# Reading all 47 block experts into TensorE's registers during the second shared chunk instead of one per routed block

## What is computed

```
shared = (silu(x @ sfc1.T) * (x @ sfc2.T)) @ sfc3.T        # 256 -> 512 -> 256
top_w, top_idx = top_k(x @ gate_w.T, 2);  top_w = softmax(top_w)
h   = silu(einsum('td,ehd->teh', xf, w1))                  # 256 -> 128 per expert
moe = einsum('teh,te,edh->td', h, dispatch, w2)            # 128 -> 256 per expert
x   = x + tanh(g_ffn[3]) * (moe + shared)
```

## Time and profile before

| what | value |
|---|---|
| runs | 2107.64, 2121.74, 2106.2 us |
| median | 2107.64 us |
| span of the profiled execution | 2103.8 us |
| mean granted TensorE clock in it | 0.915 |
| TensorE matmul busy | 1757.4 us, 84% |
| VectorE busy | 1144.3 us, 54% |
| ScalarE busy | 890.7 us, 42% |
| GpSimd busy | 861.0 us, 41% |

### The profile page before, as it was taken

One profiled execution on the slowest core, in us unless ns is written; L12 is line 12 of the kernel. 1 busy time (PEld: TensorE's weight loads), 2 busy tenths in 40 slices (PEclk: granted clock), 3 DMA queues, 4 the chain that ended last, 5 costly groups with the idle time before them and its releaser, 6 DMA issues.

```text
span 2103.8 us, 25825 instructions
## 1 busy us (share of the span) xinstructions
PE 1757.4 (84%) x9054; PEld 1079.5 (51%) x9054; DVE 1144.3 (54%) x2206; ACT 890.7 (42%) x1397; POOL 861.0 (41%) x810
## 2 busy tenths in 40 slices
PE   6936999959867888839996987999999999967985
PEld 3426899837643222434553664544555554543652
DVE  5742544478795776722225696556565556452224
ACT  3312443323378877611212664555544445410530
POOL 2162112124595544430004463566565566725022
PEclk9767999989987999969998987999999999989997
DMA  9531322020000000340113000000000000022442
GB/s 354 182 101 55 119 100 100 19 100 1 20 1 1 6 6 5 124 171 28 37 36 98 1 1 31 1 1 0 1 1 1 1 1 1 1 88 83 135 129 83
DMA packets 62742, 116.75 MB, mean 55 GB/s; under 512 B 8240, under 2 KB 51492, under 8 KB 60057
## 3 DMA queue, kind: packets, MB, share of 16 engines
q1 hardware_dynamic: 54552, 94.92, 13.0%
q0 software_dynamic: 8064, 20.19, 2.9%
HBM read 71.22 MB, written 44.89 MB: 55 GB/s over the span
## 4 chain that ended last, share of the span: by engine, by line
PE 64%; DVE 14%; ACT 6%; POOL 6%; issue 5%; another core or an unknown queue 3%; DMA 2%; SPq 0%; POOLq 0%; ACTq 0%; DVEq 0%
PE psum L151 61%; POOL arena L1777 3%; DVE arena L2311 2%; ACT arena L1567 2%; DVE arena L156 1%; POOL xb L1030 1%; DVE arena L2375 1%; DVE arena L172 1%; DMA arena<-xb 1%; POOL arena L1786 1%; DVE arena L2318 1%; DVE rounded L898 1%; PE psum L667 1%; DVE arena L1155 1%
## 5 line engine op out<-in xcount | busy, mean ns | idle before, releaser
L151 PE MATMUL psum<-arena 128*64 128x512 f32 (+21 forms) x5109 | 1191.5, 463 | 178.2 <-issue 24.9
L151 PEld LDWEIGHTS psum<-arena 128*128 128x128 f32 (+8 forms) x5109 | 569.1, 165 | 684.8 <-issue 465.9
L151 PE MATMUL psum<-rounded 128*128 128x270 f32 (+6 forms) x2688 | 486.0, 334 | 27.6 <-DVE rounded L898 19.6
L151 PEld LDWEIGHTS psum<-rounded 128*128 128x128 f32 (+3 forms) x2688 | 379.1, 187 | 134.6 <-issue 44.8
L2403 POOL TENSOR_TENSOR arena<-arena 128x1024 f32<-128x1024 f32 (+1 forms) x112 | 265.8, 2374 | 133.8 <-ACT arena L2353 131.6
L2353 ACT ACTIVATE arena<-psum 128x1024 f32<-128x1024 f32 x144 | 147.4, 1024 | 172.0 <-PE psum L151 171.3
L2311 DVE TENSOR_REDUCE arena<-psum 128x1 f32<-128x512 f32 x256 | 163.6, 682 | 90.4 <-PE psum L151 89.3
L1567 ACT ACTIVATE arena<-psum,arena 128x1024 f32<-128x1024 f32 (+1 forms) x192 | 156.5, 911 | 46.5 <-PE psum L151 46.4
L850 POOL DMA_INDIRECT arena<-yb,arena x48 | 46.1, 960 | 266.3 <-DMA yb<-arena 252.8
L1793 POOL TENSOR_TENSOR arena<-arena 128x256 f32<-128x256 f32 x128 | 95.8, 770 | 117.7 <-ACT arena L1567 116.9
L1183 POOL DMA_INDIRECT yt<-arena x40 | 39.9, 998 | 208.0 <-DVE arena L1146 205.8
(11 more groups left out here) (268 smaller groups left out, 1951.8 us busy)
## 6 DMA issues: line engine op xcount, KB each, us to landing
arena<-in_w SPq DMA_DIRECT2D x8, 2048.0 KB, 7.8
arena<-xb SPq DMA_DIRECT2D x70, 128.0 KB, 2.2
yb<-arena SPq DMA_DIRECT2D x70, 128.0 KB, 1.7
arena<-in_w1u SPq DMA_DIRECT2D x4, 2048.0 KB
xb<-arena SPq DMA_DIRECT2D x3, 2048.0 KB, 15.9
xb<-arena SPq DMA_DIRECT2D x2, 2064.0 KB, 32.6
arena<-xb SPq DMA_DIRECT2D x8, 516.0 KB
yt<-arena SPq DMA_DIRECT2D x2, 2048.0 KB, 16.6
```

Of the source, the lines that this page charges most:

```text
L151: return e.matmul(o, l, r, start=start, stop=stop, skip_group_check=True)
```

## The change

`pe_shared` takes an additional argument `between`, a function that it calls after each `mm`. For chunks 0, 2 and 3 it does nothing. For chunk 1 it is `next_expert`, which loads the next entry of `ER` into a register of its own: 16 calls fall behind the up matmuls and 16 behind the down matmuls. The 15 entries that are left are loaded after the chunk, one behind another, ahead of the wait for `s_hs` and of `turn(0)`. The first call waits for `s_er`, a wait that stood ahead of the loop before. In the loop, `up(j)` loads nothing any more; `up` and `down` use the same register values as before. No other engine's stream is changed.

```diff
--- before.py
+++ after.py
@@ -2585,7 +2585,7 @@
                     e.dma_start(yb3[128 * (j - 2):128 * (j - 2) + 128, :], f3_Y[:, (j - 2) % 3, :]).then_inc(
                         s_rout[(j - 2) % 3], 16)
 
-        def pe_shared(e, c):
+        def pe_shared(e, c, between=lambda: None):
             for f in range(4):
                 n = 4 * c + f
                 b1 = 2 * (n % 2) + 2
@@ -2596,6 +2596,7 @@
                     for k in range(2):
                         m = mm(e, psum[:, b1 + i, :], w[:, k, 128 * f:128 * f + 128], XT[:, k, 512 * c:512 * c + 512],
                                k == 0, k == 1)
+                        between()
                     m.then_inc(s_up, 1)
             for t in range(4 * c, 4 * c + 4):
                 e.wait_ge(s_hs, 4 * c + 4)
@@ -2647,8 +2649,20 @@
             pe_totals(e, 16, 32, f3_w)
             e.wait_ge(s_w3, 32)
             e.wait_ge(s_slot, 5)
-            for c in range(2):
-                pe_shared(e, c)
+            pe_shared(e, 0)
+            regs = []
+
+            def next_expert():
+
+                if len(regs) < NB3:
+                    if not regs:
+                        e.wait_ge(s_er, 2)
+                    n = len(regs)
+                    regs.append(e.value_load(ER[0:1, n:n + 1], min_val=0, max_val=15))
+
+            pe_shared(e, 1, next_expert)
+            while len(regs) < NB3:
+                next_expert()
 
             def turn(j):
                 e.wait_ge(s_rin[j % 4], RIN3[j % 4] + 16 * (j // 4 + 1))
@@ -2662,7 +2676,6 @@
                 e.wait_ge(s_bx, 23 + j + 1)
                 if j >= 2:
                     e.wait_ge(s_bh_, 23 + j - 1)
-                regs[j] = e.value_load(ER[0:1, j:j + 1], min_val=0, max_val=15)
                 for k in range(2):
                     m = mm(e, psum[:, 2 + j % 2, 0:128], f3_XGT[:, j % 3, k, :],
                            f3_W1[:, bass.ds(regs[j], 1), k, :].rearrange("p e n -> p (e n)"), k == 0, k == 1)
@@ -2680,12 +2693,10 @@
                 mm(e, psum[:, 6 + j % 2, 0:256], f3_HTT[:, j % 2, :],
                    f3_W2[:, bass.ds(regs[j], 1), :].rearrange("p e n -> p (e n)"), True, True).then_inc(s_bd, 1)
 
-            regs = {}
             e.wait_ge(s_hs, 8)
             turn(0)
             turn(1)
             e.wait_ge(s_wm, 208)
-            e.wait_ge(s_er, 2)
             for j in range(NB3 + 2):
                 if j < NB3:
                     up(j)
```

## The result

| | kernel before | changed kernel |
|---|---|---|
| median of 16 runs each | 2108.38 us | 2118.85 us |
| lowest to highest | 2102.69 to 2121.74 | 2112.25 to 2127.26 |
| span of the profiled execution | 2103.8 us | 2116.0 us |

The ratio of changed to before is 1.0041, with a 95% interval of 1.0023 to 1.0059: 8.6 us slower, 4.8 to 12.4. The medians are 10.5 us apart. The forecast of 2118 and its sign hold. All ratios in this document leave out two disturbed executions of over 4000 us, one of the kernel before and one of e6.

A forecast was written before the change was run, and what follows sets the result against it. TensorE's sequencer, with one register load a block, was taken to bound the routed blocks. Moved loads 14.7 plus clock 2.7 minus loop gain 7.3 gave 10.1 us later, span 2113.9, forecast 2118 us; range for all 2107 to 2126.

The forecast's parts named there:

- What bounds the blocks before: In the 47 routed blocks, TensorE's sequencer with one register load a block sets the pace, 1.59 us on average.
- What is late next: In the blocks without loads, row loads queued behind stores on SP: 4.04 us per three blocks, 1.35 a block.
- The gain: In the block loop: 46 x (1.53 - 1.35) - 1.0 = 7.3 us saved, bounds zero and 17.8.
- What the moved loads cost: In and behind the second shared chunk: 0.65 us a load, so the blocks begin 14.7 us later; bounds 9.1 and 18.1.
- 16 loads behind the up matmuls cost nothing: In the second shared chunk, 0.65 us a load fits under a 0.86 us matmul pair; without cover 10.4 us.
- The clock: First blocks: about 10 us idle cools the array to half clock for 5.4 us, costing 2.7; bounds nothing and 5.4.
- Nothing behind the blocks changes: Behind the last block: gathers move with the blocks' end, so its gain or loss passes on unchanged.
- The sum: Whole kernel: 14.7 + 2.7 - 7.3 = 10.1 us later, all on the path, a span of 2113.9.
- overlapping loads: Rival, in the 31 loads behind 1943.61: only 0.17 us paid each, blocks start no later, 2100 us; chance 0.06.
- blocks that stay near 1.59: Rival, in the loop: values don't stay in registers or landings lengthen, no gain, 2125 us; chance 0.12.
- a clock of 1.2 GHz through the blocks: Rival, in the blocks: TensorE stays at 1.2 GHz, 38 us more, 2150 us or over; chance 0.05.
- a block bound by the array: Rival, in the blocks: array binds at 1.20 to 1.30 us, not rows; 2107 to 2115, named 2111; chance 0.17.

The follow-up runs named there:

- e6: Kernel before, each block's expert load without its run-time bounds check (no register arithmetic or assertion): 2066.43 us against 2070.26, ratio 0.9980.
- e4: Kernel before, with each row load in SyncE's stream issued one step earlier: 2106.58 us, ratio 0.9984.
- e3: Changed kernel, with each row load in SyncE's stream issued one step earlier: 2112.32 us against the changed kernel's 2118.85.
- clean pair: Kernel before and changed kernel, both unedited, run again under other conditions: 2069.26 and 2078.95 us, ratio 1.0046.
- e2: Changed kernel, 47 loads placed elsewhere: 12 behind first chunk's up matmuls, 19 ahead of its last tile, 16 behind second chunk's up matmuls: 2116.92 us, ratio 1.0040.
- e5: Changed kernel, with the run-time bounds check of each loaded expert left out: 2072.63 us, ratio to the kernel before 1.0006.
- e7: Kernel before, all 47 experts read by three multi-register loads without bounds check ahead of the first turn: 2073.62 us, ratio 1.0015.
- e8: Changed kernel, an unread dummy matmul call behind each of the last 15 loads: one execution, S to end 182.77 us against 182.45.
- e12: Same kernel as e2, no edit, run again under the other conditions: 2074.43 us, ratio to the kernel before 1.0019.
- first group: Profiles taken under one group of conditions; under the other, every kernel that ran in both was 38 to 43 us shorter.
- e11: Kernel before, with e6's load without bounds check and e4's earlier row loads: 2055.04 us against 2069.26, ratio 0.9919.

## Why the prediction was right, point by point

- **What bounds the blocks before** (the sequencer): right. e6 takes only sequencer work out and gains 5.6 us; e4 makes rows earlier and gains 2.9.
- **What is late next** (rows, 4.04 us per three blocks): right. It is 4.10 between the turns at 2008.37, 2012.47 and 2016.57, and e3 takes this limit away and reaches 1.26 a block. The mean is 1.42 with the long landings. The gain, 7.3 forecast, was 7.7 and, in the clean pair, 7.45. So near a hit is in part luck: in the five other kernels whose blocks load no expert and keep the order of the row loads (e2, e5, e7, e8, e12) the blocks take 65.9 to 68.4 us, a gain of 4.6 to 7.0 over the kernel before of the same group. Their length goes with TensorE's waits for rows: its weight loads wait 7.0 us in the changed kernel (65.27) and 10.8 in e2 (68.44). I had charged 1.0 us for the long landings and not asked what makes them. The traces tell: they show 322 row loads of the blocks with their landings. In flight with 58 of them was a packet of 16384 bytes that the profile calls "instruction", on queue 8. Those loads took 2.9 us in the median and up to 4.1, and all 25 landings over 3.1 us are among them; the other 264 took 2.2 in the median and 3.03 at most. The DMA table of the window of the load at 2004.73, which took 3.60, has the packet (queue: packets, MB, share):

```profile
q8 instruction: 1, 0.02, 2.2%
```

- **What the moved loads cost**: 14.7 forecast from 0.65 a load, 13.75 to 13.9 measured. The pace was right (0.65). The term is 0.8 to 0.95 too large: 20.74 us lie between the first down matmul at 1949.70 and the first turn's at 1970.44, where I had counted 21.5. The 15 loads behind the chunk took 9.76, as forecast, but the down matmuls with their 16 loads 11.0 and not 16 x 0.72 + 0.2 = 11.7. And in the kernel before there are 7.0 us between the two matmuls (1943.61 and 1950.62), where I had taken 6.8 by the turn's weight load.
- **16 loads behind the up matmuls cost nothing**: right. In the clean pair all of the 13.92 us to the first turn is in the hand-over.
- **The clock**: the gap cooled the array, but the cost was 1.05 us by the third sigmoid and at most 1.4 by the seventh, and not 2.7. This term was mis-sized, by two steps. The stretch at 0.50 was 3.4 us long and not 5.4, which varies (3.4 to 5.6 in the table under e8). And a cold block was priced at twice its array time, half of the stretch, where the table shows about a third of it. Part of the first blocks is spent waiting for other engines, such as ScalarE's copy at 1971.14, from the end of the first turn at 1971.12 to the first up matmul at 1971.79; that such waits hide the rest of the price is argued, not shown.
- **Nothing behind the blocks changes**: right, 77.68 and 77.72; 53.78 and 53.79.
- **The sum**: 10.1 forecast. The two pairs of profiles give 7.0 and 6.6 from S on, the medians 10.5 and 9.7, the ratios' intervals, turned into us, 4.8 to 12.4 and 5.4 to 13.5. In the clean pair the 3.5 us that the sum is too large are 0.8 of the moved loads, 0.15 of the loop, and 2.55 of the clock: only 0.15 of the cold start shows ahead of the first sigmoid, and the rest of it is inside the net 7.45. That the median hit the forecast to a microsecond is luck of scatter. The 3 us between profiles and medians weren't found in the last stage and stay open.
- **The rivals**: overlapping loads are out (0.65 apart), and so are blocks that stay near 1.59 (1.42) and a clock of 1.2 GHz through the blocks (1.00 from 3.4 us on). So is a block bound by the array (1.20 to 1.30); it came only with the rows' order changed.

## What to carry to other kernels

A register load is sequencer time, 0.65 us with its bounds check and 0.36 without. Here a pair of matmuls of 512 columns (0.86 us) hid it and a pair of 256 columns (0.44 us) didn't, so a third of the moved loads was covered, and the 31 others cost more than 47 loads saved. Before moving such work, look for what can be left out of it, and for what is late next, because the two limits lowered together gave 13 us in the blocks where each alone gave 3 and 6. And a gap in one profile isn't free room until it is known what makes it.

## What the runs showed of the hardware

- Waits of 11 us (VectorE), 30 us (ScalarE) and 35 us (the chain of the earlier trace rows) beside the scatters and the gathers were there in the first group and absent in the second, with the same kernel. From S to the end the kernel before took 216.46 us with them and 175.81 without. TensorE crept at 0.70 us per instruction in e2 among them. The theory that these are instruction fetches held up behind the indirect DMAs isn't borne out by the traces: in none of the six profiles of the first group is there a packet of a queue that the profile calls "instruction" between S and 50 us behind it, and so none landed when a wait beside the scatters or the creep ended. What decides between the groups is open; the chip is one of the things that differed.
- A row load with a 16384-byte instruction packet in flight landed in 2.9 us in the median and up to 4.1, without one in 2.2 and at most 3.03 (322 loads in 14 profiles).
- A load of 16 registers takes 3.80 us, 12.6 times a load of one, so one instruction for many saves the check, the gaps and 0.06 us a register.
- With its row loads issued a block earlier, a landing took 2.7 us in the median at 1.26 us a block (e3), 2.5 at 1.30 (e11), and 2.2 at 1.53 (e4), as without that edit. So the earlier issue alone doesn't lengthen it; that the faster pace of loads and stores does is argued.
- After gaps of 5.1 to 9.8 us without matmuls the granted clock was 0.50 for 3.4 to 5.6 us behind the first turn, which cost 1.05 to 1.94 us up to the third block, about a third of the cold stretch.
